# Values of two key blocks in one piece on TensorE, in a cross-attention and feed-forward kernel

## The reference, cut to what matters

```python
x = x + xattn(layernorm(x), ctx, mask, ...)
#   q = w8a8_linear(x, wq, bq)        (rows quantised to 127 steps)
#   k = cond @ wk.T + bk ; v = cond @ wv.T + bv
#   scores = einsum('bhnd,bhld->bhnl', q, k) / sqrt(D) + mask
#   attn = softmax(scores) ; o = einsum('bhnl,bhld->bhnd', attn, v)
#   return w8a8_linear(o, wo, bo)
x = x + ffn(layernorm(x), ...)
#   down(silu(gate(x)) * up(x)), 1408 hidden, weights (int - 128) * scale
```

## Time and profile before

| | |
|---|---|
| median of 3 executions | 542.67 us (540.88 to 545.26) |
| profiled execution | 544.36 us, of which the span of the trace is 542.5 |
| mean granted clock of TensorE | 0.974 of full |
| TensorE busy | 486.7 us, 90% |
| VectorE busy | 379.0 us, 70% |
| ScalarE busy | 262.8 us, 48% |
| GpSimd busy | 257.6 us, 47% |

### The profile page before, as it was taken

The page is one execution under the profiler, slowest core; times in us unless marked ns, Lnnn a source line. Parts: engine busy times, 40 slices in busy tenths (PEclk is TensorE's granted clock), DMA queues, the critical chain, the costliest instruction groups (busy, mean ns, idle before and its releaser), DMA issues.

```text
span 542.5 us, 6902 instructions
## 1 busy us (share of the span) xinstructions
PE 486.7 (90%) x2377; PEld 304.1 (56%) x2377; DVE 379.0 (70%) x480; ACT 262.8 (48%) x460; POOL 257.6 (47%) x132
## 2 busy tenths in 40 slices
PE   5898678889899999999999988998989999889994
PEld 3686456568554444444444434342438878768883
DVE  2879861878757777677768886786787677565444
ACT  3538831521256657566566746558754213312220
POOL 3005700702139878798787768758551111112120
PEclk9998989989969999999999989999999999999998
DMA  7797989689196734527090720003032533353422
GB/s 232 269 326 278 330 241 277 240 242 262 61 207 202 153 62 103 112 56 159 2 213 2 153 61 2 2 2 116 1 117 80 163 128 116 109 186 133 162 72 77
DMA packets 44388, 77.41 MB, mean 143 GB/s; under 512 B 5280, under 2 KB 13504, under 8 KB 44352
## 3 DMA queue, kind: packets, MB, share of 16 engines
q1 hardware_dynamic: 44352, 76.94, 48.8%
HBM read 57.95 MB, written 18.87 MB: 142 GB/s over the span
## 4 chain that ended last, share of the span: by engine, by line
PE 51%; DVE 18%; issue 7%; ACT 4%; DMA 4%; SPq 1%; POOL 1%; POOLq 0%; ACTq 0%; DVEq 0%
PE ps L784 10%; PE ps L804 8%; PE ps L754 7%; DVE neg_m L1275 6%; PE ps L892 6%; PE ps L893 6%; DVE p_sum L1414 3%; PE ps L911 3%; PE ps L912 3%; PE ps L704 2%; DMA v_d<-v_st 2%; ACT p_t L1053 2%; PE ps L631 1%; PE ps L632 1%; PE ps L633 1%
## 5 line engine op out<-in xcount | busy, mean ns | idle before, releaser
L1275 DVE TENSOR_REDUCE neg_m<-ps 128x1 f32<-128x1024 f32 x128 | 152.9, 1220 | 55.3 <-PE ps L754 55.2
L1053 ACT ACTIVATE p_t<-ps 128x512 f32<-128x512 f32 x256 | 140.2, 600 | 80.2 <-PE ps L784 77.8
L1572 POOL TENSOR_TENSOR p_sum<-p_sum,p_t 128x1024 f32<-128x1024 f32 x46 | 112.6, 2460 | 10.5 <-ACT p_t L1053 8.8
L784 PE MATMUL ps<-q_st,k_st 97*128 97x512 f32 x256 | 102.6, 448 | 5.5 <-ACT p_t L1053 4.6
L1572 POOL TENSOR_TENSOR p_sum<-p_t 128x1024 f32<-128x1024 f32 x30 | 78.7, 2641 | 56.8 <-ACT p_t L1053 56.8
L784 PEld LDWEIGHTS ps<-q_st,k_st 97*128 97x128 f32 x256 | 46.3, 193 | 83.1 <-ACT p_t L1053 63.7
L754 PE MATMUL ps<-k_st,q_st 96*128 96x512 f32 x256 | 84.6, 412 | 6.1 <-DVE neg_m L1275 4.2
L1581 POOL TENSOR_TENSOR q_st<-v_gr,k_st 128x512 fp32r<-128x512 f32 x22 | 28.4, 1290 | 104.9 <-ACT k_st L1149 104.9
L1531 POOL TENSOR_TENSOR v_st<-v_st,bv_bc 128x512 f32<-128x512 f32 x16 | 23.9, 1512 | 103.2 <-ACT v_st L1010 103.2
L892 PE MATMUL ps<-xt_hi,k_st 128*128 128x512 f32 x176 | 69.4, 394 | 1.4 <-DVE xt_lo L1374 1.4
L804 PE MATMUL ps<-p_t,v_gr 128*32 128x512 f32 x512 | 69.9, 619 | 0.8 <-ACT p_t L1053 0.7
(11 more groups left out here) (116 smaller groups left out, 633.0 us busy)
## 6 DMA issues: line engine op xcount, KB each, us to landing
k_st<-k_hi_d SPq DMA_DIRECT2D x16, 512.0 KB, 6.9
mask_sb<-in_mask SPq DMA_DIRECT2D x3, 2048.0 KB, 10.8
w_int<-in_w_gate SPq DMA_DIRECT2D x22, 256.0 KB, 2.8
w_int<-in_w_up SPq DMA_DIRECT2D x22, 256.0 KB, 3.0
w_int<-in_w_down SPq DMA_DIRECT2D x22, 256.0 KB, 3.5
raw<-in_ctx_t SPq DMA_DIRECT2D x16, 256.0 KB, 6.8
k_hi_d<-kq_hi SPq DMA_DIRECT2D x16, 256.0 KB, 5.0
k_lo_d<-kq_lo SPq DMA_DIRECT2D x16, 256.0 KB, 6.4
```

Of the source, the lines that this page charges most:

```text
L784: mm = pe.matmul(ps[:, bank, :], k_st[g % SLOTS][0:rows, j, P * lc:P * lc + P], q_st[g % SLOTS][0:rows, j, :], start=True, stop=not with_mask)
L1053: act.activation(p_t[:, q % 4, j, :], ps[:, score_bank(lc, j), :], ACT.Exp).then_inc(exp_done, 1)
L1275: dve.tensor_reduce(neg_m[:, g % 2, nt, j:j + 1], ps[:, bank:bank + 2, :], AX_XY, ALU.max, negate=True).then_inc(max_read, 1)
L1572: pool.tensor_tensor(total, former, p_t[:, q % 4, hs, :], ALU.add).then_inc(added_pool, 1)
```

## The change

TensorE takes the attention steps in pairs. The values of two blocks stand together at the end of the odd step, of the blocks three and two before it (before: one block a step, the one just before, in the middle of the step). The four units of a pair are spread anew: one in the even step, three in the odd one, the last behind the values. Both sets of sums of the former group stand together directly behind the values of lc = 1 (before: lc = 1 and lc = 2), and in RING "U" stands ahead of the last unit of that step. After "U" the slots go on alternating (HOLD = 1). The turning moves from lc = 4 to lc = 3. ScalarE's two output copies move to the second and the fourth exp of lc = 1. The last two blocks' values stand together at the end. VectorE's, GpSimd's and SyncE's programs keep their order but for the turning.

```diff
--- before.py
+++ after.py
@@ -303,9 +303,9 @@
 
 
         SET = 4
-        SUM_LC = 2
-        TURN_LC = 4
-        HOLD = PER_STEP + 1
+        SUM_LC = 1
+        TURN_LC = 3
+        HOLD = 1
 
 
         OUT_BANK = 7
@@ -348,9 +348,10 @@
         RING += [("R", 0)] + [("M", 1, u) for u in range(AHEAD)]
         for g in range(G):
             for lc in range(LC):
-                RING += sum(ring_of_step(g, lc), [])
-                if g >= 1 and lc == SUM_LC - 1:
-                    RING.append(("U", g - 1))
+                units, rows, turned, tail = ring_of_step(g, lc)
+                if g >= 1 and lc == SUM_LC:
+                    units = units[:-1] + [("U", g - 1)] + units[-1:]
+                RING += units + rows + turned + tail
 
 
         slot_of, slot_before, latest, slot = {}, {}, [None, None], 0
@@ -694,16 +695,18 @@
             pe.wait_ge(flag_ready, 2)
             masked = pe.value_load(mflag_i[0:1, 0:1], min_val=0, max_val=1)
 
-            def sums(g, k):
+            def sums(g):
 
                 bank, _ = ring_banks(("U", g))
-                i = LC // SET * g + k
-                for half in range(2):
-                    pe.wait_ge(*added[SET * i + SET - 1, half])
-                for j in range(HG):
-                    mm = pe.matmul(ps[D * j:D * j + D, bank, :], ones[:, :], p_sum[:, i % TOTALS, j // 2, j % 2, :],
-                                   start=(k == 0), stop=(k == LC // SET - 1))
-                mm.then_inc(sum_done, 1)
+                for k in range(LC // SET):
+                    i = LC // SET * g + k
+                    for half in range(2):
+                        pe.wait_ge(*added[SET * i + SET - 1, half])
+                    for j in range(HG):
+                        mm = pe.matmul(ps[D * j:D * j + D, bank, :], ones[:, :],
+                                       p_sum[:, i % TOTALS, j // 2, j % 2, :],
+                                       start=(k == 0), stop=(k == LC // SET - 1))
+                    mm.then_inc(sum_done, 1)
 
             def turn_output(g):
 
@@ -830,27 +833,33 @@
                     pe.wait_ge(d_rows, 16 * HG * (g + 1))
                     for lc in range(LC):
                         units, rows, turned, tail = ring_of_step(g, lc)
-                        units = iter(units)
-
-                        def next_unit():
+                        if lc % 2 == 0:
+                            units_of_pair = iter(units + ring_of_step(g, lc + 1)[0])
+
+                        def next_unit(units=units_of_pair):
                             key = next(units, None)
                             if key is not None:
                                 if key[2] == 0:
                                     wait_operands(key[1])
                                 max_unit(*key[1:])
 
-                        scores(g, lc, (0, 1))
-                        next_unit()
-                        scores(g, lc, (2,))
-                        if quad(g, lc) >= 1:
-                            weighted_values(*divmod(quad(g, lc) - 1, LC))
-                        scores(g, lc, (3,))
-                        next_unit()
-                        if g >= 1 and lc == SUM_LC - 1:
-                            ring(("U", g - 1))
-                            sums(g - 1, 0)
-                        elif g >= 1 and lc == SUM_LC:
-                            sums(g - 1, 1)
+                        if lc % 2 == 0:
+                            scores(g, lc, (0, 1, 2))
+                            next_unit()
+                            scores(g, lc, (3,))
+                        else:
+                            scores(g, lc, (0,))
+                            next_unit()
+                            scores(g, lc, (1, 2))
+                            next_unit()
+                            scores(g, lc, (3,))
+                            for q in (quad(g, lc) - 3, quad(g, lc) - 2):
+                                if q >= 0:
+                                    weighted_values(*divmod(q, LC))
+                            if g >= 1 and lc == SUM_LC:
+                                ring(("U", g - 1))
+                                sums(g - 1)
+                            next_unit()
                         if rows:
                             max_rows(g + 1)
                         if turned:
@@ -859,6 +868,7 @@
                         for key in tail:
                             for k, bank in enumerate(ring(key)):
                                 tail_content(0, key[1], key[2] + k, bank)
+                weighted_values(G - 1, LC - 2)
                 weighted_values(G - 1, LC - 1)
 
             with pe.If(masked != 0):
@@ -922,8 +932,7 @@
                     if n >= 1:
                         down(n - 1)
                     if n == 0:
-                        for k in range(LC // SET):
-                            sums(G - 1, k)
+                        sums(G - 1)
                 elif kind == "output":
                     take_place(p)
                     turn_output(G - 1)
@@ -1111,9 +1120,9 @@
                 for lc in range(LC):
                     for j in range(HG):
                         exps(g, lc, j)
-                        if g >= 1 and (lc, j) == (0, HG - 1):
+                        if g >= 1 and (lc, j) == (1, 1):
                             copy_out(g - 1, 0)
-                        elif g >= 1 and (lc, j) == (SUM_LC + 1, 0):
+                        elif g >= 1 and (lc, j) == (SUM_LC, HG - 1):
                             copy_out(g - 1, 1)
                     if g == OT + 1 and lc < 2:
                         scale_output(0, 2 * lc)
```

## The result

The changed kernel takes 555.89 us (median of 4, 552.09 to 560.37) where the kernel before takes 542.52: a ratio of 1.0246, interval 1.0188 to 1.0303. It is slower by 2.5%. The forecast was 530.9, and the range ended at 538.5.

A forecast was written before the change was run, and what follows sets the result against it. TensorE was taken as the bound, with GpSimd second. Gains over the groups summed to 13.5 us, less 1.7 for the clock: 11.8 off the median of 542.67 gave 530.9 us, range 525.0 to 538.5.

The forecast's parts named there:

- The walk over TensorE: Step-by-step timing of an ordinary attention group's pairs: 27.7 us against 30.35, a gain of 2.65 per group.
- 0.33 per change between wide and tiled work: TensorE pays 0.33 us per tiled piece; 47 fewer pieces in attention save 15.5 us, 2.0 per ordinary group.
- ScalarE's three banks: Scores wait for exps to free three score banks, taking 0.14 to 0.19 us of the 0.33 saved per pair.
- the waits that go: TensorE's waits at sums, group start, rows and turning: of 2.0 us per group, 1.5 go at once.
- Rival B: The change between blocks is still paid inside a double piece, up to 0.33 us each: 544.5 us, no change; chance 0.09.
- A: Rival: ScalarE's three banks take all that pairing saves, a pair is 6.14 us, the kernel 536.8; chance 0.18.
- the term of VectorE's add: In a group's first pair, the add of a set's last block runs 3.6 to 4.9, sums at 5.3: 0.4 us spare.
- Rival C: Sums wait behind VectorE's add and GpSimd's stretched second set, with clock drops, 3.6 us per group: 556 us; chance 0.06.
- Groups 5 to 7: Last three attention groups: gains of 1.8 and 2.0 us in groups 5 and 6, a loss of 2.5 in group 7.
- The clock as an amplifier: One more stretch of 3.4 us at the lower clock, in group 7, charged as 1.7 us lost.

The follow-up runs named there:

- e1: Changed kernel with VectorE's add of a set's last block moved between the two maxima of the even step: 538.17 us, ratio 0.9927 to the kernel before.
- e4: Changed order in groups 0 to 4 only, with the add between the maxima there; order before in groups 5 to 7: 534.62 us, ratio 0.9823.
- e5: Changed kernel with VectorE's adds of groups 0 to 6 left out, so work is missing: 539.05 us, ratio 0.9877 to the kernel before.
- e7: Changed order in groups 0 to 6, order before in group 7, add between the maxima: 535.67 us, ratio 0.9859 to the kernel before.
- e9: Changed kernel, order untouched, VectorE's add in groups 0 to 6 replaced by a one-input maximum over the same elements: 536.56 us, ratio 0.989.
- e11: e4 again with more executions: 536.0 us, ratio 0.9801 to the kernel before.
- e10: e1 with the pair's last unit put between the two blocks' values, so each is its own tiled piece: 545.03 us, ratio 1.0065 to the kernel before.
- e6: Changed kernel with VectorE's add moved ahead of both maxima of the even step: 571.17 us, ratio 1.0487 to the kernel before.
- e2: Kernel before, with only VectorE's add moved late, behind the first maximum of the odd step: 569.73 us, ratio 1.0524.
- e3: Changed order in groups 0 to 4 only, order before in groups 5 to 7, add not moved: 542.09 us, ratio 0.9995 to the kernel before.

## Why the prediction was wrong

- **The walk over TensorE held.** 0.33 per change between wide and tiled work, ScalarE's three banks, the waits that go: it gave 27.7 for an ordinary group, and e1, e4, e5, e7, e9 and e11 give 27.74 to 27.80. Its parts in e1 are 7.83, 6.91, 6.55 and 6.50 for the pairs with sums, with turning, with rows and the last, where it had 7.69, 6.97, 6.84 and 6.2. Rival B is out (no gap in 16 records; e10), and so is A, by which the group would be 28.5.
- **The step that failed is the term of VectorE's add**: "Its add of a set's last block is now behind a unit that comes in the odd step, which puts it at 3.6 to 4.9 ...; the sums stand at 5.3. In time by 0.4." I placed it rightly (it begins 3.67 after the pair's first score), and the walk has GpSimd's set start "when the exps of step 1 or 5 are there", which the trace shows at 3.51. I still costed the add at 1.22, as if the two engines were apart. It measured 3.29. Together with the two maxima behind it, that put back 3.0 us in each ordinary group: 1.8 at the rows (8.64 for 6.84), 1.1 at the sums (8.77 for 7.69), 0.2 in the last pair. Moving the add alone (e1) shortens the groups by 20.6 us in the profiles, 14.2 of it in groups 0 to 4.
- **Rival C had the place and not the mechanism.** It had the sums wait behind the add and GpSimd's set, at 3.6 us a group, if GpSimd stretched. GpSimd's adds of 2.4 stayed at 2.4, but for the one that waits in its turn. It was VectorE that stretched, and the larger wait was at the rows. That C's 556 is the measured time is luck: its sum had a drop of the clock in each of seven groups, and groups 1 to 4 have none. Its 0.06 was far too little: the kernel before showed adds of 3.30, and its groups by line gave L1414 18 instructions and 26.0 us, a mean of 1442 ns where the ordinary one is 1.22 us. A mean 0.2 us above the common value was the sign.
- **Groups 5 to 7.** Forecast were gains of 1.8 and 2.0 and a loss of 2.5. With the add cured (e1) they lose 1.5, 0.7 and 4.3. Group 7's reason fits the traces (scores bunched with no maxima between, ScalarE's square root), and e7 shows the order to be the cause. I had forecast the fall of the clock there too, but not its size: I charged one stretch of 3.4 us at the lower level, and the changed kernel has 10.6 us in group 7. The loss of group 5 in e1 goes with one more stretch at the lower clock: e7 has the same order and add there, takes 36.1 as before, and has a granted clock of 0.95 where e1 has 0.91. What makes up the 0.7 of group 6 wasn't taken apart.
- **The clock as an amplifier** I had as a fixed charge of 1.7. Over the whole span the granted clock is 0.937 in e6 and 0.964 in e1, so 35.8 and 19.2 us of work are lost to it (568.4 x 0.063, 534.6 x 0.036): 16.6 of the 33.8 us between the two profiled executions. In e2 it is 0.957, 24.3 us against 14.1 before: 10 of 22.5. In e2 and e6 the lower level often followed a stop of 1.2 to 1.9 us, but not each time, and in groups 1 to 4 of the changed kernel stops of 1.93 to 2.65 us were followed by none. What decides it, these runs don't show.

## What to carry to other kernels

Before an instruction of VectorE with two inputs in on-chip memory is moved, lay GpSimd's timeline beside it: with GpSimd's adds the two exclude each other, and a 1.2 us add costs what is left of GpSimd's instruction on top. Put it into a gap of GpSimd's, or take one input from PSUM if it is there anyway. A form with one input helps only if its own row shows it: the reduction was not touched, the conversion to bf16 was. When the shortest, median and mean of a line differ, look at the long ones before you use the common one as a price.

## What the runs showed of the hardware that I had not expected

- An add of VectorE over 128x1024 floats takes 1.22 us alone, and 3.29, 2.86 or 2.42 when it begins 0.16, 0.61 or (in e6, into the second of two) 1.1 us after the start of one of GpSimd's adds: until GpSimd's current instruction ends, and then 1.1 more, in 96 of 96 cases. GpSimd's next instruction then waits in its turn (5.67 us for two, and not 4.70).
- A maximum over the same elements of the same tensor, with one input, isn't touched (1.207 to 1.220 in 14 of 14), nor is an add with one input in PSUM (0.69). A conversion from float to bf16, with one input, is (2.76 for 0.69).
- The same order of instructions can run into the collision or miss it, by where GpSimd happens to be (group 0: adds of 1.25 to 1.47 in e3, of 3.28 in the changed kernel).
- Sixteen column-tiled records of two accumulations into one bank run on as one piece: 1.92 us, against 1.06 for eight.
